# A Strassen-like autoencoder kernel: recombination by accumulating DMAs, first and last pieces cut, and weight sums of two steps in one instruction

## The reference

```python
f     = relu(einsum('bld,ldf->bf', x, W_enc) + b_enc)      # x: (512, 2, 1024), W_enc: (2, 1024, 4096)
x_hat = einsum('bf,lfd->bld', f, W_dec) + b_dec            # W_dec: (2, 4096, 1024), all float32
```

## Time and profile before

| | us |
|---|---|
| median of three runs | 693.49 |
| profiled execution | 693.06 |
| its span, first to last instruction | 691.3 |
| PE busy | 649.4 (94%) |
| DVE busy | 599.0 (87%) |
| ACT busy | 339.2 (49%) |
| DMA, mean of the 16 engines | 56.9%, 184 GB/s |

### The profile page before, as it was taken

The page is one execution under the profiler, slowest core; times in us unless marked ns, Lnnn a source line. Parts: engine busy times, 40 slices in busy tenths (PEclk is TensorE's granted clock), DMA queues, the critical chain, the costliest instruction groups (busy, mean ns, idle before and its releaser), DMA issues.

```text
span 691.3 us, 7987 instructions
## 1 busy us (share of the span) xinstructions
PE 649.4 (94%) x2888; PEld 527.4 (76%) x2888; DVE 599.0 (87%) x773; ACT 339.2 (49%) x423; POOL 0.7 (0%) x6
## 2 busy tenths in 40 slices
PE   2989999999999999999999999998979998989996
PEld 0867888888878888888888888876757876767885
DVE  4999989879999858579994999999999999999844
ACT  3455335354564444556566665454444453454452
POOL 0000000000000000000000000000000000000000
PEclk9999999999999999999999999999999999999999
DMA  8966675665566564647455665654545554445524
GB/s 300 306 186 187 199 223 182 203 191 165 157 199 204 179 197 138 197 137 224 141 191 175 185 211 185 206 189 136 183 146 159 183 182 140 159 143 181 191 101 181
DMA packets 66518, 126.90 MB, mean 184 GB/s; under 512 B 4784, under 2 KB 4784, under 8 KB 66480
## 3 DMA queue, kind: packets, MB, share of 16 engines
q1 hardware_dynamic: 66480, 126.40, 56.9%
HBM read 122.18 MB, written 4.19 MB: 183 GB/s over the span
## 4 chain that ended last, share of the span: by engine, by line
PE 68%; DVE 25%; issue 4%; DMA 1%; ACT 1%; SPq 0%; DVEq 0%; ACTq 0%
PE sums L502 22%; PE sums L504 22%; PE sums L503 22%; DVE w_split L321 9%; DVE w_raw L321 5%; DVE place L321 5%; DVE forms L321 3%; PE sums L514 3%; DVE s_sum L321 3%; DMA w_raw<-w_enc 1%; ACT place L270 0%; ACT place L282 0%; ACT forms L250 0%; ACT w_split L232 0%; ACT forms L248 0%
## 5 line engine op out<-in xcount | busy, mean ns | idle before, releaser
L502 PE MATMUL sums<-w_split,forms 128*128 128x512 f32 x896 | 357.4, 399 | 34.8 <-DVE w_split L321 26.9
L232 ACT CAST w_split<-w_raw 128x1024 fp32r<-128x1024 f32 (+1 forms) x256 | 240.2, 945 | 297.1 <-PE sums L504 219.2
L504 PE MATMUL sums<-w_split,forms 128*128 128x512 f32 x896 | 352.0, 393 | 0.0
L503 PE MATMUL sums<-w_split,forms 128*128 128x512 f32 x896 | 351.8, 393 | 0.0
L321 DVE TENSOR_TENSOR w_split<-w_raw,w_split 128x1024 fp32r<-128x1024 f32 (+1 forms) x256 | 268.8, 1086 | 61.1 <-ACT w_split L232 61.0
L502 PEld LDWEIGHTS sums<-w_split,forms 128*128 128x128 f32 x896 | 169.8, 189 | 81.1 <-issue 29.6
L504 PEld LDWEIGHTS sums<-w_split,forms 128*128 128x128 f32 x896 | 169.8, 190 | 36.1
L503 PEld LDWEIGHTS sums<-w_split,forms 128*128 128x128 f32 x896 | 170.1, 190 | 33.5
L321 DVE TENSOR_TENSOR w_raw<-w_raw 128x512 f32<-128x512 f32 x256 | 176.2, 688 | 9.2 <-DMA w_raw<-w_enc 4.8
L321 DVE TENSOR_TENSOR place<-place,sums 128x1024 f32<-128x1024 f32 x28 | 32.5, 1214 | 8.1 <-PE sums L504 8.1
L321 DVE TENSOR_TENSOR place<-place 128x1024 f32<-128x1024 f32 x28 | 33.1, 1218 | 0.0
(11 more groups left out here) (16 smaller groups left out, 47.7 us busy)
## 6 DMA issues: line engine op xcount, KB each, us to landing
w_raw<-w_enc SPq DMA_DIRECT2D x96, 512.0 KB, 5.0
w_raw<-w_dec SPq DMA_DIRECT2D x96, 512.0 KB, 4.5
w_raw<-w_enc SPq DMA_DIRECT2D x32, 256.0 KB, 3.0
w_raw<-w_dec SPq DMA_DIRECT2D x32, 256.0 KB, 2.7
place<-xT SPq DMA_DIRECT2D x9, 512.0 KB, 7.6
outT<-place SPq DMA_DIRECT2D x16, 256.0 KB, 2.2
b_enc_sb<-b_enc SPq DMA_DIRECT2D x1, 16.0 KB, 8.8
b_dec_sb<-b_dec SPq DMA_DIRECT2D x1, 8.0 KB, 9.3
```

The source lines that it names most:

```text
L232: nc.scalar.copy(split(s, q, 0), w_pos(s, 2 * q, n)).then_inc(hi_done, 1)
L502: nc.tensor.matmul(out, v_hi, w_hi, start=k == 0, stop=False)
L503: nc.tensor.matmul(out, v_lo, w_hi, start=False, stop=False)
L504: last = nc.tensor.matmul(out, v_hi, w_lo, start=False, stop=k == PAIRS - 1)
```

## The change

There are four edits.

1. **Weight sums for two steps.** `w_sums(s + 1, 2)` is issued at odd steps s alone, and one instruction then covers the same tile of steps s + 1 and s + 2 (128 x 2 x 512). It waits for the loads of both. `hi` of tiles 0 and 1 waits for the first of the three sums, no longer for all.
2. **Recombination by DMA.** In `dec2` and `dec3` two `take_out`s remain, those that read PSUM. The five that were in SBUF alone are DMAs that add to their destination, issued by GpSimd (`fold`): 512 KB each, five after each of chunks 10 to 13, twenty in all. ACT copies some banks with the sign turned, and the buffer `V_PLACE` comes in.
3. **Pieces at the start.** The first `x` and weight tiles are loaded as six DMAs of 256 KB, and the first product begins with the first pieces. There are 12 warming matmuls in place of 8.
4. **Pieces at the end.** PE orders the last two steps by product: product 0 of both, then 1 of both, then 2 of step 126, four tiles of transposes, product 2 of step 127, and the last four tiles.

```diff
-    SUMS = {"enc1": 3, "enc2": 4, "dec1": 0, "dec2": 7, "dec3": 7, "dec4": 4}
+    SUMS = {"enc1": 3, "enc2": 4, "dec1": 0, "dec2": 2, "dec3": 2, "dec4": 4}
+    FOLDS = {"enc1": 0, "enc2": 0, "dec1": 0, "dec2": 5, "dec3": 5, "dec4": 0}
-             "dec2": [(True, 1), (True, 2), (False, 1), (False, 3)],
+             "dec2": [(True, 1), (True, 2), (False, 1), (False, 2)],
...
+            first_x, first_w = whole(X_PLACE[0]), slice(0, C)
+            sp.dma_start(first_x[:, 0, :], x_pairs[:, 0, 0, :]).then_inc(piece_loaded[0], 16)
+            sp.dma_start(w_pos(0, 0), w_enc[0:P, 0, first_w]).then_inc(piece_loaded[1], 16)
...
+            def fold(dst, src):
+                pool.dma_start(whole(dst), whole(src), accum_op=ALU.add).then_inc(folded, 16)
...
+                pool.wait_ge(copied, COPIED[n + 1])
+                fold(y11, U2)
+                pool.wait_ge(summed, SUMMED[n + 1])
+                fold(U3, V_PLACE)
+                fold(y21, V_PLACE)
+                pool.wait_ge(folded, FOLDED[n] + 48)
+                fold(y12, U3)
+                fold(y22, U3)
...
-                act.wait_ge(w_sums_done, W_SUMS[s + 1])
+                act.wait_ge(w_sums_done, W_SUMS[s + 1] if q or s < 2 else W_SUMS[s - s % 2] + 1)
...
-                nc.scalar.copy(whole(dst), banks(p)).then_inc(copied, 1)
+                negative = kind != "enc1" and dst in (y22, U3)
+                nc.scalar.activation(whole(dst), banks(p), ACT.Copy,
+                                     scale=-1.0 if negative else 1.0).then_inc(copied, 1)
...
-            def w_sums(s):
+            def w_sums(s, n=1):
+                def pos(p):
+                    return w_raw[:, s % RAW:s % RAW + n, p * C:(p + 1) * C]
+                for t in range(s, s + n):
+                    dve.wait_ge(w_loaded[t % RAW], 32 * (t // RAW + 1))
...
+                add(pos(dst), pos(dst), pos(src)).then_inc(w_sums_done, 1)
+                add(pos(3), pos(3), pos(1)).then_inc(w_sums_done, 1)
+                add(pos(2), pos(2), pos(3)).then_inc(w_sums_done, 1)
...
-                if s + 1 < STEPS:
-                    w_sums(s + 1)
-                lo(s, 0)
+                if s == 0:
+                    w_sums(1)
+                elif s % 2 and s + 1 < STEPS:
+                    w_sums(s + 1, 2)
+                if s:
+                    lo(s, 0)
...
-                multiply(s)
+                if s < STEPS - 2:
+                    multiply(s, range(4 if FOUR[s] else 3))
+                elif s == STEPS - 2:
+                    multiply(s, [0])
+                    multiply(s + 1, [0])
...
+            multiply(STEPS - 2, [1])
+            multiply(STEPS - 1, [1])
+            multiply(STEPS - 2, [2])
             for j in range(8):
+                if j == 4:
+                    multiply(STEPS - 1, [2])
```

More of the change, by code:

```diff
@@ L50, in autoencoder_kernel @@
     COPIES = {"enc1": 3, "enc2": 0, "dec1": 3, "dec2": 2, "dec3": 2, "dec4": 0}
-    SUMS = {"enc1": 3, "enc2": 4, "dec1": 0, "dec2": 7, "dec3": 7, "dec4": 4}
+    SUMS = {"enc1": 3, "enc2": 4, "dec1": 0, "dec2": 2, "dec3": 2, "dec4": 4}
+    FOLDS = {"enc1": 0, "enc2": 0, "dec1": 0, "dec2": 5, "dec3": 5, "dec4": 0}
+    FOLDED = [16 * sum(FOLDS[ch[1]] for ch in CHUNKS[:n]) for n in range(len(CHUNKS) + 1)]
     COPIED = [sum(COPIES[ch[1]] for ch in CHUNKS[:n]) for n in range(len(CHUNKS) + 1)]
@@ L104, in autoencoder_kernel @@
         x_loaded = [sem(f"x_loaded{i}") for i in range(PAIRS + 1)]
+        piece_loaded = [sem(f"piece_loaded{i}") for i in range(3)]
+        begun_hi = sem("begun_hi")
+        begun_lo = sem("begun_lo")
         bias_loaded = sem("bias_loaded")
@@ L197, in store @@
                     sp.dma_start(outT[row:row + P, :], place[:, src:src + 2, :]).then_inc(stored, 16)
-            for s in range(RAW):
+            first_x, first_w = whole(X_PLACE[0]), slice(0, C)
+            sp.dma_start(first_x[:, 0, :], x_pairs[:, 0, 0, :]).then_inc(piece_loaded[0], 16)
+            sp.dma_start(w_pos(0, 0), w_enc[0:P, 0, first_w]).then_inc(piece_loaded[1], 16)
+            sp.dma_start(first_x[:, 1, :], x_pairs[:, 0, 1, :]).then_inc(x_loaded[0], 16)
+            sp.dma_start(w_pos(0, 1), w_enc[0:P, 1, first_w]).then_inc(piece_loaded[2], 16)
+            low = slice(PAIRS * P, (PAIRS + 1) * P)
+            sp.dma_start(w_pos(0, 3), w_enc[low, 1, first_w]).then_inc(w_loaded[0], 16)
+            sp.dma_start(w_pos(0, 2), w_enc[low, 0, first_w]).then_inc(w_loaded[0], 16)
+            for s in range(1, RAW):
                 load_x(s, X_PLACE[s], x_loaded[s])
@@ L222, in _ @@
                                     base=0, pattern=[[-1, P]], channel_multiplier=1).then_inc(ident_set, 1)
+            def fold(dst, src):
+                pool.dma_start(whole(dst), whole(src), accum_op=ALU.add).then_inc(folded, 16)
+            for n, (_, kind, _, _, _) in enumerate(CHUNKS):
+                if not FOLDS[kind]:
+                    continue
+                y11, y12, y21, y22 = out_place(n)
+                pool.wait_ge(copied, COPIED[n + 1])
[6 more added lines that the diff above has]
+                fold(y22, U3)
         @block.scalar
@@ L411, in take_out @@
                         dve.wait_ge(copied, COPIED[n])
+                        dve.wait_ge(folded, FOLDED[n])
                         dve.wait_ge(multiplied, ready + 3)
-                        op = add(y21, y22 if first else y21, banks(2))
-                    elif k == 2:
+                        op = add(y21, y22 if first else y21, banks(2), sub)
+                    else:
                         dve.wait_ge(copied, COPIED[n + 1])
-                        op = add(y11, y11, u2)
-                    elif k == 3:
@@ L418, in take_out @@
                         dve.wait_ge(multiplied, ready + 4)
[L419 to L429, removed]
+                        op = add(v, banks(3), u2, sub)
@@ new lines, in _ @@
+            form_sums(0, 0)
+            dve.wait_ge(piece_loaded[2], 16)
+            add(w_pos(0, 1), w_pos(0, 1), w_pos(0, 0)).then_inc(w_sums_done, 1)
+            dve.wait_ge(form_hi, 1)
+            add(forms[:, 0, 1, 2, :], place[:, at + kh + 1, :], forms[:, 0, 0, 2, :].bitcast(F32),
+                ALU.subtract)
+            form_lo_sums(0, 0)
+            dve.wait_ge(hi_done, 1)
+            add(split(0, 0, 1)[:, C:2 * C], w_pos(0, 1), split(0, 0, 0)[:, C:2 * C].bitcast(F32),
+                ALU.subtract).then_inc(lo_done, 1)
@@ L475, in _, with multiply @@
         def _(pe):
-            def multiply(s):
+            def multiply(s, products):
                 n, k = s // PAIRS, s % PAIRS
                 r, kind, four, c, _ = CHUNKS[n]
-                if c == 0:
+                if c == 0 and s > 0:
                     pe.wait_ge(form_lo, form_counts(r, k))
-                for p in range(4 if four else 3):
+                for p in products:
                     q = p // 2
-                    if p % 2 == 0:
+                    if s == 0 and p == 0:
+                        pe.wait_ge(begun_lo, 2)
+                    elif s == 0 and p == 1:
+                        pe.wait_ge(form_lo, 1)
+                        pe.wait_ge(lo_done, 1)
+                    elif p % 2 == 0:
                         pe.wait_ge(hi_done, 2 * s + q + 1)
```

72 lines of the change are left out of this document (49 added, 23 removed).

## The result

The changed kernel takes 739.18 us (median of 4 runs, 738.08 to 740.11), the kernel before 693.38 us. The ratio is 1.0653, with a 95% interval of 1.0631 to 1.0675: slower by 46 us. The forecast was slower by 19.4, 713 us, with a range from 699 to 728. The direction was right, and the time lies outside the range.

The account below looks back on a forecast made before the run. TensorE (PE), busy for 649.4 of 691.3 us, was taken to bound the kernel. The terms 22.8 - 1.0 + 1.8 - 8.2 + 4 + 0 = +19.4 us gave 712.5, stated as 713 us, range 699 to 728.

Parts of the forecast that it names:

- The loop: Chunks 1 to 3: load, three wide sums, two `lo` take 12.3 us per two steps against PE's 10.88; +20.4 us.
- The folds: Chunks 10 to 13: traffic of accumulating DMAs lengthens loads in the loop; taken as +4 us, between 0 and 16.
- Rival one, folds in full: Folds hit two loop loads in each chunk at full 2.8 us: +12 us, 723 to 728 us; chance 0.18.
- chunk 4, "one sum less each two steps 1.0 come back": Chunk 4: of 1.3 us now lost to DVE, one sum less each two steps gives back 1.0.
- chunk 10, "+2.4": Chunk 10 runs in the loop, 4 x 11.6 = 46.4 us; +2.4 us, counting the step until its slack is gone.
- chunks 11 to 13: Decoder: loop and `take_out` stalls give 47.5, 49.8 and 46.7 us, changes of -2.0, -2.8 and -2.5.
- chunk 14: Decoder: DVE has four `take_out`s of 1.14 us less, -3.3 us.
- chunk 15 and the end, "0" and +0.2: Chunk 15: a wide sum ahead of `lo` at k = 1 adds 0.2 us; the end adds 0.
- The low clock: Chunk 12: after PE's 4.7 us stall, mostly 1.2 GHz, 11 matmuls in 4 us, 1.5 us lost.
- Chunk 0: Chunk 0: head start spent at step 3's load and the wide block; step 7's `lo` done at 65.9; +2.7 us.
- The end: Last matmuls, transposes and stores: no net change, 0 us, between -1 and +1.
- The recombination: Chunks 10 to 14: recombination by DMA, less the loop, gives -8.2 us together.

Follow-up runs that it names:

- late_block: The changed kernel with the block of wide sums of an odd step moved behind that step's two `lo`: 673.34 us, ratio 0.9697.
- small_folds: The changed kernel with each fold cut to 64 of 512 columns, all waits kept: 720.55 us, ratio 1.0381.
- pairs_only: The kernel before with the weight sums for two steps alone: 732.87 us, ratio 1.0544.

## Why the prediction was right and wrong, step by step

**The loop (right).** Load, three wide sums, two `lo`: 12.3 us said, 12.0 measured in the turn shown, 12.4 over the three chunks; chunks 1 to 3 at 50.3 said, 50.1 measured; chunk 4's start at 221.2 said, 220.4 measured. `late_block` shows it as the cause. DVE waited 116 us for weight loads, where 40 or more had been said. The rule of the Trainium skill for a DMA's time ("DMA: Bandwidth & Descriptors", section "Anatomy of one DMA — SWDGE (gpsimd) path") would have had no loop (10.4 us, an estimate by its figures, against 10.88); second DMAs that land after 5.7 us and fifty waits for loads decide against it for these loads.

**The folds (wrong, this step sinks the forecast).** The step read: "each keeps the 16 engines as long as half a 1 MB load does, some 2.8 us, and two of five fall on a load in the loop, three chunks: 16 us. I take +4, near the lower end, since the engines are free half the time". Measured: 18.6 us by the medians, 21.0 by the profiles of chunks 11 to 14. In the three chunks that the step counts it was 12.6, inside its bounds and three times the +4 that I took; the other 8.4 are chunk 14, to which it gave nothing. A mean share of 0.5 says nothing of the moment at which loads and folds meet: in chunk 11 the second `take_out` starts at 493.7 us, two folds are issued at 495.3 and 495.8, and the next load at 496.1 and 496.5. The second DMAs of the loads from 494 to 500 us, first in the changed kernel, then in `small_folds`:

```profile
DMA to landing us min/median/max: 9.7/10.0/10.2
...
DMA to landing us min/median/max: 5.0/5.2/5.4
```

So beside folds a load lands some 5 us later, not 2.8, and this happens to two loads in each of chunks 11 to 13 and to four in chunk 14. There the second DMA (line 194) of the loads from 652 to 671 us, and that of the kernel before (line 183, 583 to 660 us), landed after:

```profile
DMA to landing us min/median/max: 6.6/8.4/10.7
...
DMA to landing us min/median/max: 3.8/4.2/4.8
```

PE pays for it where it waits for `lo`: 4.3, 2.9, 2.6 and 7.0 us in chunks 11 to 14, against 0.6, 0.8, 0 and 1.0 in `small_folds`. Taking the value nearest to nothing was not a reading of a row. Rival one, folds in full, had the right mechanism, and its 728 still lies 11 us below the result. What the Trainium skill says in "DMA: Bandwidth & Descriptors", section "Issuing engines are not separate DMA queues", was borne out: GpSimd's DMAs lengthened those of SP, from 5.2 to 10.0 us.

**The rest of the miss.** The profiled execution moved by 739.81 - 693.06 = 46.75 us, and 19.4 were said. Of the 27.3 between, the folds' size explains 14.6 by the medians, and 18.0 by the two profiled executions (739.81 - 717.82 - 4). (The run of `small_folds` that was profiled is the fastest of its four, so the truth lies between.) The other 9.3 stand in the chunks of `small_folds`, which leaves most of the folds' bytes out:

| Step of the prediction | said, us | measured, us |
|---|---|---|
| chunk 4, "one sum less each two steps 1.0 come back" | 33.0 | 35.7 |
| chunk 9, not spoken of | 33.1 | 34.3 |
| chunk 10, "+2.4" | 46.7 | 47.8 |
| chunks 11 to 13 | 144.0 | 147.3 |
| chunk 14 | 34.4 | 34.1 |
| chunk 15 and the end, "0" and +0.2 | 46.4 | 47.6 |

In chunk 4 I counted only the saved sums. The changed kernel's first turn there, block to block, is 11.3 us of DVE work (three `take_out`s and activation work) with no wait for a load, and the next two are 8.4 us each, behind waits of 1.7 and 2.8 us: the loop of three-product steps, put at 8.4 us against 8.16, binds. In chunk 9 the last block belongs to chunk 10: 1 MB to load and three wide sums, in front of `lo` for which PE gives 8.16 us. It costs 1.2 us here, 3.7 in the changed kernel and 6.2 in `pairs_only`, with the same code at that place. In the latter two PE came back at a lower clock; why the wait for this load differs (1.3, 2.2 and 3.5 us) is not shown.

**The low clock (undersized).** I counted it once, in chunk 12. In the changed kernel it came after ten of the eleven stalls of more than 2.5 us, and once after one of 1.8 us: the starts of the matmuls then stand 0.43 us apart in place of 0.23. PE stalled until 511.8 us and ran at half the clock (0.50) until 517.9, 15 matmuls in 6.1 us; across its return to full speed:

```profile
514.50:520.30 5.80, 5.80 (x20) 4.64 (x19) 5.31 (x8) 1.05 (x1) 0.00 (x0) 0.71 0.95 306
```

20 matmuls in 5.8 us, where 25 fit at the upper level, 2.4 GHz. In chunks 1 to 3 the time comes out right without it, so there it is hidden behind DVE. In chunks 11 to 14 it accounts for some 8.3 of the 21.0 us between the changed kernel and `small_folds`, by PE's busy time.

**Chunk 0 (right).** The blocks of wide sums were to start at 22.0, 34.8, 47.6 and 59.9 us, and started at 21.7, 34.8, 47.4 and 59.4; both `lo` of step 7 were done at 65.4, 65.9 said. So the early start is spent at step 3's load. Without pairs chunk 0 ends at 65.0 us in place of 67.7.

**The end (inside its bounds).** 0 said, between -1 and +1; about +0.9 by the profiles.

**The recombination (its gain too small).** -8.2 with the loop was right within some 4 us (`small_folds`, chunks 10 to 14); that without the loop it would give 19.4 us I had not worked out.

## What to carry to other kernels

When an instruction is made wider by reaching ahead, write down the loop that it closes: what it waits for, what stands behind it on its engine, and which of those frees the buffer for the next load. The period of that loop, not the saved work, is what the edit costs; moving the block behind the instructions that free the buffer opened it here, at no cost. A transfer that is harmless where loads have two steps to land is not where they have one, so two edits that measured alone are worth -19 and +39 us are worth +46 together (the ends, about -1 by themselves, included), and the traffic of a burst must be set against the moment it comes, not against the mean share of the queues.

## What the runs showed of the hardware

- An accumulating DMA of 512 KB from SBUF to SBUF landed after 7.7 us (median), a plain copy of the same bytes after 5.2, one of 64 KB with accumulation after 4.5, all issued by GpSimd beside weight loads. In the first two GpSimd's queue (`software_dynamic` in the profile) had the same 2880 packets, and they took 7.6% and 3.9% of the engines' time.
- Beside such folds the second DMA of a 1 MB weight load landed 9.7 and 10.2 us after its issue, where it was 5.0 and 5.4 beside folds of 64 KB; the mean DMA share of the chunk was 0.75.
- A weight sum over two buffers, 128 x 2 x 512, costs what 1024 columns in a row cost: 1.22 us each, three in a block of 3.66.
- PE's granted clock fell to half after a stall of 1.8 us (chunk 9) and after ten of eleven stalls of more than 2.5 us, for 7 to 14 matmuls each time.
